# First attention, pass for the row maxima: three score buffers, and the next head's rows turned in quarters on two shared banks

## What is computed

```python
D, N_HEADS, d_head = 256, 16, 16
scale = 1.0 / np.sqrt(np.sqrt(d_head))
Q = (X @ Wq.T + bq).reshape(B, S, H, d_head) * scale      # S = 1024
K = (X @ Wk.T + bk).reshape(B, S, H, d_head) * scale
V = (X @ Wv.T + bv).reshape(B, S, H, d_head)
scores = jnp.einsum('bqhd,bkhd->bhqk', Q, K)
scores = jnp.where(causal[None, None], scores, -jnp.inf)
attn = jax.nn.softmax(scores.astype(jnp.float32), axis=-1)
out = jnp.einsum('bhqk,bkhd->bqhd', attn, V).reshape(B, S, D)
return out @ Wo.T + bo
```

## Time and profile before

| | us |
|---|---|
| median of 3 runs | 1867.23 |
| lowest, highest | 1865.87, 1867.99 |
| the profiled execution's time | 1864.84 |
| its span | 1863.1 |
| its mean granted TensorE clock | 0.923 of full speed |

### The profile page before, as it was taken

One profiled execution on the slowest core, in us unless ns is written; L12 is line 12 of the kernel. 1 busy time (PEld: TensorE's weight loads), 2 busy tenths in 40 slices (PEclk: granted clock), 3 DMA queues, 4 the chain that ended last, 5 costly groups with the idle time before them and its releaser, 6 DMA issues. The chain is left out here.

```text
span 1863.1 us, 39066 instructions
## 1 busy us (share of the span) xinstructions
PE 1552.3 (83%) x14453; PEld 1069.3 (57%) x14453; DVE 1205.6 (65%) x2406; ACT 861.8 (46%) x2356; POOL 738.2 (40%) x1048
## 2 busy tenths in 40 slices
PE   5877983297444899999999999999999999749998
PEld 2443342264322666766776677677667767635554
DVE  6776127732555778778778887877888786333443
ACT  2223851142133666666656656665665664311111
POOL 6000000375114356656645665564566565400000
PEclk9998996598767999999999999998999999869999
DMA  7000004085522556465545646464564654110111
GB/s 231 1 2 2 2 1 141 24 268 169 158 60 54 120 138 166 102 158 138 150 113 136 166 109 158 130 152 109 138 166 102 160 135 113 52 40 28 39 38 44
DMA packets 226773, 196.38 MB, mean 105 GB/s; under 512 B 87202, under 2 KB 203810, under 8 KB 224544
## 3 DMA queue, kind: packets, MB, share of 16 engines
q1 hardware_dynamic: 218720, 180.35, 36.8%
q0 software_dynamic: 3456, 9.43, 1.6%
q10 hardware_dynamic: 4416, 4.20, 0.7%
HBM read 121.79 MB, written 72.03 MB: 104 GB/s over the span
## 5 line engine op out<-in xcount | busy, mean ns | idle before, releaser
L1600 PE MATMUL d_big<-all_xn_t,all_w 128*128 128x512 f32 x512 | 262.2, 638 | 45.8 <-DVE d_conv L1818 39.2
L1818 DVE SCALAR_TENSOR_TENSOR d_conv<-d_big,all_cw,d_conv 128x1023 f32<-128x1023 f32 (+2 forms) x192 | 245.6, 1279 | 70.2 <-ACT d_conv L1982 66.2
L1600 PEld LDWEIGHTS d_big<-all_xn_t,all_w 128*128 128x128 f32 x512 | 93.2, 199 | 124.0 <-issue 83.1
L2168 POOL TENSOR_TENSOR d_y<-d_y,all_xn 128x256 f32<-128x256 f32 x128 | 105.2, 822 | 126.1 <-DVE d_y L1961 66.8
L1789 PE MATMUL d_big<-all_wo,d_yt 128*128 128x256 f32 x512 | 127.6, 395 | 12.5 <-DVE d_yt L1888 12.5
L2082 ACT COPY d_ys<-d_big 128x128 f32<-128x128 f32 x256 | 62.5, 267 | 157.7 <-PE d_big L1751 137.8
L2374 PE MATMUL e_gu<-all_xn_t,all_last_up 128*128 128x512 f32 x272 | 122.2, 603 | 12.6 <-DVEq L2402 12.6
L1722 PE MATMUL d_big<-all_w,all_xn_t 128*128 128x256 f32 x512 | 126.0, 390 | 0.1
L2125 POOL TENSOR_TENSOR d_vs<-d_vs,d_sv 128x1024 f32<-128x1024 f32 x32 | 61.3, 1915 | 152.6 <-DMA d_vs<-turned_v_scratch 151.4
L1862 DVE SCALAR_TENSOR_TENSOR d_AI<-d_big,d_b_col,d_decay 128x256 f32<-128x256 f32 x256 | 104.6, 476 | 20.6 <-PE d_big L1613 19.8
L324 DVE TENSOR_REDUCE a_neg_max<-a_big 128x1 f32<-128x128 f32 (+7 forms) x128 | 90.0, 752 | 32.3 <-PE a_big L257 31.9
(11 more groups left out here) (359 smaller groups left out, 3733.3 us busy)
## 6 DMA issues: line engine op xcount, KB each, us to landing
turned_kq_scratch<-d_turned SPq DMA_DIRECT2D x32, 512.0 KB, 4.0
d_kq_tok<-turned_kq_scratch SPq DMA_DIRECT2D x128, 128.0 KB, 3.4
turned_v_scratch<-d_vs SPq DMA_DIRECT2D x16, 1024.0 KB, 5.0
d_vs<-turned_v_scratch SPq DMA_DIRECT2D x64, 256.0 KB, 6.5
grouped_y_scratch<-d_yx SPq DMA_DIRECT2D x32, 512.0 KB, 3.0
d_yx<-grouped_y_scratch SPq DMA_DIRECT2D x128, 128.0 KB, 3.6
all_w<-in_L_attn_W_qkvz SPq DMA_DIRECT2D x16, 768.0 KB
l_hold<-in_L_ffn_gate_up_proj SPq DMA_DIRECT2D x48, 192.0 KB, 3.4
```

What stands on the lines that cost most here:

```text
L1600: mm = pe.matmul(big[0][:, c, :], w_sb[par][:, k, n * DK:(n + 1) * DK], xn_t[:, k, c * 512:(c + 1) * 512], start=(k == 0), stop=(k == KD - 1))
L1818: dve.scalar_tensor_tensor(conv[:, sh:T], src[:, 0:T - sh], cw[:, bass.ds(g, 1), COLUMN_OF[j], 3 - sh], conv[:, sh:T], ALU.mult, ALU.add). ...
L2168: pool.tensor_tensor(part, part, zs[:, t, :], ALU.mult).then_inc(s["yg_s"], 1)
```

## The change

The scores go round `big[2]`, `big[3]` and `big[1]`, three buffers for the tiles in one running count, where there were two. Each turn is cut into quarters of 512 tokens (3 matmuls of 512 columns), with one ScalarE copy of 112 x 512 each. Quarters, values and turned maxima are listed in the order in which TensorE issues them (`side`), and go by turns into the two banks of `big[0]`; each waits until what stood two places earlier in the list has been read (`free`). In the order of TensorE the four quarters of the next head stand after tiles 1, 2, 3 and 4. The diff, cut to its core:

```diff
--- before.py
+++ after.py
@@ -189,6 +189,15 @@
         block = blk_setup.enter_context(nc.Block())
         UNITS = [(n, mt) for mt in range(KD) for n in range(2)]
         unit_ps = [big[2], big[3], big[0], big[1]]
+        NBUF = 3
+        score_buf = [big[2], big[3], big[1]]
+        side = [("turn", 0, quarter) for quarter in range(4)]
+        for h in range(H0):
+            side += [("turn", h + 1, quarter) for quarter in range(4 if h + 1 < H0 else 0)]
+            side += [("values", h)] if h < TT else []
+            side += [("maxima", 0)] if h == HALF else []
+        side += [("maxima", 1)]
+        side_at = {step: k for k, step in enumerate(side)}
 
         @block.sync
         def _(sp):
@@ -219,35 +228,44 @@
                                        xn_t[:, k, c * 512:(c + 1) * 512], start=(k == 0), stop=(k == KD - 1))
                 mm.then_inc(qk_mm, 1)
 
-            def turn(h, n):
+            def free(k):
+
+                if k < 2:
+                    if k == 0:
+                        pe.wait_ge(first_s, 6)
+                    return
+                kind, *at = side[k - 2]
+                if kind == "turn":
+                    pe.wait_ge(rows_s, 4 * at[0] + at[1] + 1)
+                elif kind == "values":
+                    pe.wait_ge(v_out, at[0] + 1)
+                else:
+                    pe.wait_ge(maxp, 4 * at[0] + 4)
+
+            def turn(h, quarter):
+                n, c = quarter // 2, quarter % 2
                 u = h // 8 * 2 + n
-                if h % 8 == 0:
+                k = side_at["turn", h, quarter]
+                free(k)
+                if h % 8 == 0 and c == 0:
                     pe.wait_ge(split_s, 3 * u + 3)
-                if h == 0:
-                    pe.wait_ge(first_s, 2 * (2 + n) + 2)
+                if h == 0 and quarter == 0:
                     pe.wait_ge(sel_set, 2 * len(SLOTS))
-                else:
-                    pe.wait_ge(rows_s, 2 * h - 1 + n)
-                if n == 0 and 1 < h < TT + 2:
-                    pe.wait_ge(v_out, h - 1)
-                if n == 0 and h == HALF + 2:
-                    pe.wait_ge(maxp, 4)
-                for c in range(2):
-                    for j in range(3):
-                        mm = pe.matmul(big[n][0:MAXROW, c, :], select[:, n, h % 8, j, :],
-                                       part[u][:, j, c * 512:(c + 1) * 512], start=(j == 0), stop=(j == 2))
+                for j in range(3):
+                    mm = pe.matmul(bank[k % 2][0:MAXROW, :], select[:, n, h % 8, j, :],
+                                   part[u][:, j, c * 512:(c + 1) * 512], start=(j == 0), stop=(j == 2))
                 mm.then_inc(turn_mm, 1)
 
             def scores(h, q):
                 i = h * TT + q
                 if q == 0:
-                    pe.wait_ge(rows_s, 2 * h + 2)
-                if i >= 2:
-                    pe.wait_ge(s_max, i - 1)
+                    pe.wait_ge(rows_s, 4 * h + 4)
+                if i >= NBUF:
+                    pe.wait_ge(s_max, i - NBUF + 1)
                 else:
-                    pe.wait_ge(first_s, 2 * i + 2)
+                    pe.wait_ge(first_s, (2, 4, 8)[i])
                 width = (q + 1) * P
-                buf = big[2 + q % 2]
+                buf = score_buf[i % NBUF]
                 for c in range((width + 511) // 512):
                     n = min(512, width - 512 * c)
                     last = c == (width - 1) // 512
@@ -260,26 +278,28 @@
 
             def values_of(t):
 
+                k = side_at["values", t]
+                free(k)
                 pe.wait_ge(w_in[2], 16)
-                pe.wait_ge(rows_s, 2 * t + 3)
-                for k in range(KD):
-                    mm = pe.matmul(bank[0][:, 0:D], xn_t[:, k, t * P:(t + 1) * P], w_t[:, 2, k, :],
-                                   start=(k == 0), stop=(k == KD - 1))
+                for d in range(KD):
+                    mm = pe.matmul(bank[k % 2][:, 0:D], xn_t[:, d, t * P:(t + 1) * P], w_t[:, 2, d, :],
+                                   start=(d == 0), stop=(d == KD - 1))
                 mm.then_inc(v_mm, 1)
 
             def turn_maxima(b):
+                k = side_at["maxima", b]
+                free(k)
                 pe.wait_ge(s_max, (b + 1) * HROW)
-                pe.wait_ge(rows_s, min(2 * ((b + 1) * HALF + 1) + 1, 2 * H0))
-                pe.transpose(bank[0][0:HROW, 0:P], neg_max[:, b * HALF:(b + 1) * HALF, :].rearrange("p h t -> p (h t)"),
+                pe.transpose(bank[k % 2][0:HROW, 0:P], neg_max[:, b * HALF:(b + 1) * HALF, :].rearrange("p h t -> p (h t)"),
                              ident[:, :]).then_inc(max_turned, 1)
 
-            turn(0, 0)
-            turn(0, 1)
+            for quarter in range(4):
+                turn(0, quarter)
             for h in range(H0):
                 for q in range(TT):
                     scores(h, q)
-                    if h + 1 < H0 and q in (2, 5):
-                        turn(h + 1, q // 3)
+                    if h + 1 < H0 and 1 <= q <= 4:
+                        turn(h + 1, q - 1)
                 if h < TT:
                     values_of(h)
                 if h == HALF:
@@ -297,11 +317,13 @@
                 act.activation(part[u][:, 0, :], flat, ACT.Identity, bias=half_bias[:, n, mt:mt + 1], scale=0.5).then_inc(first_s, 1)
                 act.activation(rest[u % 2][:, :], flat, ACT.Identity, bias=half_bias[:, n, mt:mt + 1], scale=0.5).then_inc(first_s, 1)
             for h in range(H0):
-                for n, rows in enumerate((q_rows, k_rows)):
-                    act.wait_ge(turn_mm, 2 * h + n + 1)
-                    if n == 1 and h % 4 == 0:
+                for quarter in range(4):
+                    n, c = quarter // 2, quarter % 2
+                    act.wait_ge(turn_mm, 4 * h + quarter + 1)
+                    if quarter == 2 and h % 4 == 0:
                         act.wait_ge(ones_set, h // 4 + 1)
-                    act.copy(rows[0:MAXROW, h, :], big[n][0:MAXROW, :, :].rearrange("p c n -> p (c n)")).then_inc(rows_s, 1)
+                    act.copy((q_rows, k_rows)[n][0:MAXROW, h, c * 512:(c + 1) * 512],
+                             bank[side_at["turn", h, quarter] % 2][0:MAXROW, :]).then_inc(rows_s, 1)
 
         @block.vector
         def _(dve):
@@ -321,19 +343,19 @@
 
             def maxima(h, q):
                 dve.wait_ge(s_mm, h * TT + q + 1)
-                dve.tensor_reduce(neg_max[:, h, q:q + 1], big[2 + q % 2][:, :, :].rearrange("p c n -> p (c n)")[:, 0:(q + 1) * P],
+                dve.tensor_reduce(neg_max[:, h, q:q + 1], score_buf[(h * TT + q) % NBUF][:, :, :].rearrange("p c n -> p (c n)")[:, 0:(q + 1) * P],
                                   AX.X, ALU.max, negate=True).then_inc(s_max, 1)
 
             def values_of(t):
                 dve.wait_ge(v_mm, t + 1)
-                dve.tensor_tensor(v_aug[:, t, :, 0:DH], bank[0][:, 0:D].rearrange("p (h d) -> p h d", d=DH),
+                dve.tensor_tensor(v_aug[:, t, :, 0:DH], bank[side_at["values", t] % 2][:, 0:D].rearrange("p (h d) -> p h d", d=DH),
                                   v_bias[:, :].rearrange("p (h d) -> p h d", d=DH), ALU.add).then_inc(v_out, 1)
 
             def split_maxima(b):
                 dve.wait_ge(max_turned, b + 1)
                 if b:
                     dve.wait_ge(maxp, 4)
-                turned = bank[0][0:HROW, 0:P]
+                turned = bank[side_at["maxima", b] % 2][0:HROW, 0:P]
                 dve.tensor_copy(max_part[0:HROW, b, 0, :], turned).then_inc(maxp, 1)
                 dve.wait_ge(maxp, 4 * b + 1)
                 dve.tensor_tensor(max_rest[0:HROW, 0, :], turned, max_part[0:HROW, b, 0, :], ALU.subtract).then_inc(maxp, 1)
```

## The result

The median fell from 1866.55 us (4 runs, 1863.51 to 1867.99) to 1848.51 (4 runs, 1847.57 to 1849.88): a ratio of 0.9912, 95% interval 0.9895 to 0.9929, 18.0 us less. The profiled execution has a span of 1846.3 where it had 1863.1.

The account below looks back on a forecast made before the run. It took VectorE's waits behind whole turns, with two score buffers, as the bound. Heads summed 5.87 + 8 x 6.94 + 7.69 + 5 x 6.54 + 5.6 = 107.4 us, from 125.35: 1867.2 - 18.0 = 1849.2, range 1844.5 to 1858.0.

Parts of the forecast that it names:

- Heads 10 to 14: Heads without values in the maxima pass: 6.54 us each instead of 7.56, VectorE idling ahead of tiles 3, 4, 5.
- Heads 1 to 8: Heads with values in the maxima pass: 6.94 us each instead of 7.76, a gain of 6.6 in all.
- the old walk: One head of the old order stepped through with trace durations: 7.50 us for 7.56 measured, so 0.06 was added.
- The wait for the values: In heads 1 to 8, quarter 1 waits for VectorE's addition of the values; 0.53 us idle ahead of tile 3.
- Head 15: Last head of the maxima pass, without turns: 5.6 us instead of 6.61, a gain of 1.0.
- The copies: ScalarE's 64 quarter copies instead of 32 copies, 0.59 us each, hidden behind TensorE's order and costed at nothing.
- The clock: TensorE's two clock drops, behind 44.0 and 115.9, taken as gone: head 0 at 5.87, head 9 at 7.69; 3.0 us if they stay.
- The sum: All heads of the maxima pass added up: 107.4 us instead of 125.35, a gain of 18.0.
- The third buffer without use: Rival for the score buffers: the third brings nothing, only the quarters work; about 9 us gained, 1858; chance 0.10.
- The engines' floors: Rival for the maxima pass: VectorE or TensorE never waits; pass of 92 us, gain of 33, 1834; chance 0.04.
- A clock that falls in the middle of the pass: Rival: TensorE's clock falls with more, shorter pauses, 3.4 to 4.9 us lost per head; +16, 1883 with half; chance 0.05.

Follow-up runs that it names:

- the run with the values first: The changed kernel with VectorE adding the values ahead of a head's reduction 0 instead of behind it: 1842.47 us, 0.9888 of the kernel before.
- the spread kernels: The changed kernel with quarters after tiles 1, 3, 5 and 6 instead of 1 to 4: 1836.58 us, 0.9836 of the kernel before; further variants keep these places.
- a filler: The changed kernel with two quarters' matmuls repeated into the same bank, for heads 1 and 10: 1845.80 us, 0.9894 of the kernel before.

## Why the prediction was right, point by point

Predicted were 1849.2 and a gain of 18.0; measured were 1848.51 and 18.0. The mechanism, where VectorE waits and for how long, came as predicted; the clock did not, and the last microsecond of agreement is luck.

- **Heads 10 to 14**, 6.54 predicted, 6.51 measured; idle ahead of tiles 3, 4, 5 as said (0.37, 0.29, 0.21 in the profile's count). **Heads 1 to 8**, 6.94 against 6.85. I added the 0.06 by which the old walk fell short; the new one needed none, and the walk itself was 0.03 too long. Over 8 heads the 0.09 is 0.7 too little of a gain. The wait for the values was there, and the run with the values first showed its price.
- **Head 15**, 5.6 against 5.45. **The copies**: 586 ns taken from another line's copy, 585 and 586 measured, hidden as the doubled copies showed.
- **The clock** is the step that failed. I took both drops as gone, and both stayed: head 0 took 6.81 for 5.87, head 9 9.26 for 7.69, 2.5 us together, near the 3.0 that I had priced them at. My ground for head 0 was that tile 2 and two quarters would fill the stretch ahead of 44. They ran, but from 39.53 to about 41.2, since the first turns were done 1.8 us sooner and VectorE 0.7 later; TensorE then stood for 3.29 us. For head 9 I had weighed busy time against one stretch in which nothing had fallen. The runs show that such a drop is no property of the order: head 9 fell in two of four executions with the same pauses, and head 0 kept its clock once behind a pause of 3.32. Its centre should have been a price times a chance, not nothing.
- **The sum** of the pass, 107.4, was 1.5 too low (the clock's 2.5, less 0.7 in heads 1 to 8, 0.16 in 10 to 14 and 0.15 in 15). The profiled span fell by 16.8 where I had 18.0. The medians lie 18.0 apart since the profiled execution of the kernel before was 1.7 below its median and that of the change only 0.5; where in the program these 1.2 us lie isn't shown. So the exact hit is luck in its last microsecond.
- **The rivals.** The third buffer without use is refuted by the run with two buffers: 11.6 us more of pass, of which the larger drops of the clock are less than 2 (4.1 in it against 2.5). The engines' floors weren't reached by the change; the spread kernels come close, 5.94 with TensorE busy for all of it (I had its floor at 5.88) and 5.58 against VectorE's 5.35. A clock that falls in the middle of the pass didn't come in the changed kernel. With two buffers it came once, in head 12, and cost 1.7 us. By the Trainium skill's rule (TensorE: Matmul & The Clock Gate, "A second HAM failure mode: psum-queue depth-cycling") small pauses between groups make the clock go up and down; that head agrees with it, but it is one head of 15 behind head 0, far from the price of that rival.

## What to carry to other kernels

Walk one period from the trace's durations, first the old order, to see what the walk leaves out (here 0.06 of 7.56 us), then the new: it gave seven orders of this loop within 0.1 us a head, and the eighth, with the copies twice, within 0.11. Where a long piece of work for later stands in a queue that feeds another engine, put it behind the tiles that keep that engine busy longest; here that was worth 13.6 us of pass against 16.5 of the whole change, with no buffer more. Don't forecast that a drop of the clock goes away unless the idle time ahead of it goes too; and since the same order fell in one execution and not in another, give the drop a chance and a price (here some 1 to 2 us each), and don't take one execution with a filler as proof.

## What the runs showed of the hardware

A VectorE cast of 128 x 1024 from float32 to bf16, both in SBUF, took 0.69 us alone and up to 5.31 beside GpSimd's fills; the subtractions that ran beside the fills alone took 1.22 or 1.23, those beside GpSimd's copies up to 1.61. Each of the 29 longer casts in the twelve traces started inside a fill, and each ended 0.55 behind the end of a fill. In the changed kernel the long one ran from 31.98 to 34.99 and the first fill ended at 34.44; the two of 1.38 ended at 38.99 and 42.99, the fills at 38.44 and 42.44. The cost comes back on the other side: a fill took 3.51 us alone, and 4.06 where a cast ran out its last 0.55 behind the fill's start:

```profile
34.38 4.06 POOL L216 MEMSET a_k_rows<- 32x4096 bf16 x1
...
37.61 1.38 DVE L340 CAST a0s_part<-a0s_rest 128x1024 bf16<-128x1024 f32 x1
```

The 5.31 is a cast that started inside the spread kernel's first fill and got its turn only behind the second; why it missed the change from one to the other is open. With the fills held back all four casts took 0.69.

The other way round, 14 GpSimd copies took 12.13 us where all of them ran beside VectorE's splitting, 4.36 to 5.89 where the last of them met its first subtractions, and 3.36 to 3.39 where they were all but done when the first subtraction started. The Trainium skill (SBUF — State Buffer, "Who interferes with whom") says that a cast that takes VectorE's second pair of ports and GpSimd shut each other out for a whole instruction, and that a VectorE instruction with two SBUF inputs contends with a GpSimd instruction that reads SBUF, but not with one that only writes. The 1.38, the 3.01 and the 5.31, the slow copies and the subtractions untouched by the fills agree with that.

So the start of the pass varies by 5 us (43.45 to 48.78) with the fills and the splitting unedited. From the lowest to the highest run of one kernel it is 2.3 us (the change) to 15.6 (two buffers); how much of it comes from this start isn't shown, since each kernel has one profiled execution.
